# Router logits from split half-precision outputs, with the split done by ScalarE and GpSimd

## The reference

```python
x = x + xattn(layernorm(x), ctx, ctx)          # per token: 16 heads x 16 heads, causal, softmax
xf = layernorm(x).reshape(-1, D)
logits = xf @ gate_w.T + gate_b                # router, 8 experts
top1 = argmax(logits, axis=-1)
for e in range(8):
    h = relu(xf @ w1[e].T + b1[e]); y = h @ w2[e].T + b2[e]
    out = out + where(top1 == e, y, 0)
return x + out
```

## Time and profile before

| | |
|---|---|
| time, median of 3 runs | 470.85 us (469.33 to 471.26) |
| span of the profiled execution, first to last instruction | 462.9 us |
| what lies around the span, median less span | 7.95 us |
| busy: TensorE, VectorE, GpSimd, ScalarE | 384.6, 339.8, 207.6, 181.1 us |
| start to the first scores (L1403) | 27.3 us |
| last addition to `o_sb` (L1012) | begins at 227.16 us |
| expert tiles | about 229 to 455 us |

### The profile page before, as it was taken

The page is one execution under the profiler, slowest core; times in us unless marked ns, Lnnn a source line. Parts: engine busy times, 40 slices in busy tenths (PEclk is TensorE's granted clock), DMA queues, the critical chain, the costliest instruction groups (busy, mean ns, idle before and its releaser), DMA issues.

```text
span 462.9 us, 16301 instructions
## 1 busy us (share of the span) xinstructions
PE 384.6 (83%) x5889; PEld 328.5 (71%) x5889; DVE 339.8 (73%) x777; ACT 181.1 (39%) x317; POOL 207.6 (45%) x213
## 2 busy tenths in 40 slices
PE   0126878996798969895699999898999999999991
PEld 0026767996698869894688877676788888787870
DVE  8789799789882875378676987596867677766761
ACT  2344446454542523143353433243443434434320
POOL 8536444635673548643342354743333233233321
PEclk9999999955555555565589999999999999999998
DMA  7999989889778675667552544757543443434310
GB/s 264 417 254 236 264 220 260 260 188 240 200 161 218 159 160 112 180 141 219 125 143 67 107 98 106 186 139 184 106 94 99 95 108 90 104 84 106 100 29 0
DMA packets 125802, 73.17 MB, mean 158 GB/s; under 512 B 99229, under 2 KB 110238, under 8 KB 125216
## 3 DMA queue, kind: packets, MB, share of 16 engines
q1 hardware_dynamic: 96336, 60.46, 50.6%
q0 software_dynamic: 3408, 8.46, 5.0%
q10 hardware_dynamic: 25984, 3.21, 4.9%
HBM read 48.28 MB, written 11.24 MB: 129 GB/s over the span
## 4 chain that ended last, share of the span: by engine, by line
PE 58%; DVE 12%; issue 8%; SPq 7%; POOL 6%; DMA 5%; ACT 2%; POOLq 0%; DVEq 0%; ACTq 0%
PE s_ps L1506 19%; PE at_ps L1522 7%; PE pv_ps L1522 6%; PE s_ps L1403 6%; PE pv_ps L1433 5%; PE lg_ps L1459 4%; DMA arena<-qv_hl 3%; PE at_ps L1523 3%; PE pv_ps L1523 3%; SPq L601 3%; PE tr_ps L1445 2%; DVE arena L1186 2%; PE at_ps L1420 2%; POOL sorted_rows L1340 1%; POOL qv_hl L1296 1%
## 5 line engine op out<-in xcount | busy, mean ns | idle before, releaser
L1506 PEld LDWEIGHTS s_ps<-arena 128*128 x1872 | 131.9, 99 | 43.4 <-issue 4.9
L1506 PE MATMUL s_ps<-arena 128*128 128x128 f16 x1872 | 157.0, 221 | 2.8 <-issue 1.2
L1203 DVE SCALAR_TENSOR_TENSOR arena<-arena,s_ps 128x512 f32<-128x512 f32 x78 | 53.5, 685 | 32.5 <-PE s_ps L1506 21.1
L1433 PE MATMUL pv_ps<-a_hl,arena 128*128 128x16 f16 x1536 | 54.6, 180 | 17.1 <-DMA arena<-qv_hl 12.3
L1433 PEld LDWEIGHTS pv_ps<-a_hl,arena 128*128 128x128 f16 x1536 | 53.3, 118 | 20.7 <-DMA arena<-qv_hl 16.7
L1366 POOL DMA_INDIRECT result<-arena x39 | 38.9, 996 | 64.4 <-DVE arena L1228 60.3
L1403 PEld LDWEIGHTS s_ps<-k_hl,arena 128*128 128x128 f16 x1536 | 54.5, 118 | 15.4 <-DMA arena<-qv_hl 10.6
L1522 PE MATMUL at_ps<-arena,k_in 128*128 x160 | 60.3, 379 | 2.8 <-DVE k_hl L1214 2.8
L1359 POOL TENSOR_TENSOR arena<-arena 128x256 f32<-128x256 f32 x39 | 29.5, 756 | 73.4 <-DMA arena<-b 73.3
L1403 PE MATMUL s_ps<-k_hl,arena 128*128 128x16 f16 x1536 | 54.2, 180 | 9.7 <-DMA arena<-qv_hl 9.7
L1522 PE MATMUL pv_ps<-arena,x_in 128*128 x152 | 57.6, 379 | 0.0
(11 more groups left out here) (141 smaller groups left out, 589.9 us busy)
## 6 DMA issues: line engine op xcount, KB each, us to landing
arena<-w SPq DMA_DIRECT2D x28, 512.0 KB, 5.1
arena<-sorted_rows SPq DMA_DIRECT2D x39, 130.0 KB, 2.2
arena<-b SPq DMA_DIRECT2D x39, 128.0 KB
arena<-qv_hl SPq DMA_DIRECT2D x70, 64.0 KB
k_in<-k_t SPq DMA_DIRECT2D x16, 256.0 KB
arena<-x SPq DMA_DIRECT2D x4, 1024.0 KB, 10.6
x_in<-x_t SPq DMA_DIRECT2D x16, 256.0 KB, 5.0
v_in<-v_t SPq DMA_DIRECT2D x16, 256.0 KB
```

The source lines that it names most:

```text
L1203: eng.scalar_tensor_tensor(out=h_in[:, c].rearrange("p (k t) -> p k t", t=P), in0=bias, scalar=W_SCALE, in1=h_ps[c][:].rearrange("p (k t) ...
L1433: m = eng.matmul(o[:, n], v_bd[i][:, n // 2, :, n % 2, v], a_hl[:, n, a, :], start=(n, a, v) == (0, 0, 0), stop=(n, v) == (BLK - 1, 1))
L1506: k = eng.matmul(o, weights_of(j, w + k_ * H + n * P, P), xt[:, j % XB, a + k_], start=(k_, w, a) == (0, HI_1, 0), stop=k_ == KD - 1 and w ...
```

## The change

The float32 products of `gates` become products of half-precision (float16) parts. The gate's weights are scaled by 64 and split into high and low (`gate_hl`, VectorE), and GpSimd makes `gate_bd` from both in a step of its own (`gate_blocks`). Each chunk of `o_sb` is split into `o_hl`: ScalarE copies the high part, GpSimd subtracts to get the low part. Both walk the chunk head by head, so they read float32 numbers 64 bytes apart and write float16 numbers 4 bytes apart. TensorE does three products for each head instead of one. The wait of ScalarE's split on the group before's logits takes the place of SP's: `load_residual` now waits for the two splits. `sel` is made by a product of two inputs instead of a copy. The scaling is undone in `choose`. The software DMA queue's scratch in on-chip memory is set to 2048 bytes for each partition. The order of all steps that were there before is kept; the new ones are put in behind `outputs`.

```diff
 "ACT":
+  "output_halves": (5316, 6999, 7544, 7821, 10139, 11102, 11887, 12396, 14641, 15353, 16633, 16750, 19138, 19643, 20641, 20747),
 "POOL":
+  "gate_blocks": (2900,),
+  "output_halves": (5386, 7069, 7614, 7891, 10209, 11172, 11957, 12466, 14711, 15423, 16703, 16820, 19208, 19713, 20711, 20817),
-        gate_bd = sb("gate_bd", [P, HEADS, 8, E])
+        gate_bd = sb("gate_bd", [P, HEADS, 2, 8, E], F16)
+        gate_hl = sb("gate_hl", [P, 2, HEADS * E], F16)
+        o_hl = sb("o_hl", [P, HEADS, P, 2], F16)
@@ load_residual (SP)
-                    sp.wait_ge(s_logits, i // CG)
+                    sp.wait_ge(s_o_hi, i - CG + 1)
+                    sp.wait_ge(s_o_lo, i - CG + 1)
@@ ScalarE
+            def output_halves():
+                for i in range(NC):
+                    at = slice(i % CG * BLK, (i % CG + 1) * BLK)
+                    yield
+                    act.wait_ge(s_o, i + 1)
+                    act.wait_ge(s_logits, i // CG)
+                    eng.copy(o_hl[:, :, at, 0], o_sb[:, at, :].rearrange("p t h -> p h t")).then_inc(s_o_hi, 1)
@@ constants (VectorE)
-                eng.tensor_copy(sel[:], turn_of[:].unsqueeze(2).to_broadcast([P, 8, HD])).then_inc(s_select, 1)
+                eng.tensor_tensor(sel[:], turn_of[:].unsqueeze(2).to_broadcast([P, 8, HD]),
+                                  turn_of[:].unsqueeze(2).to_broadcast([P, 8, HD]), ALU.mult).then_inc(s_select, 1)
-                dve.wait_ge(s_select, 3)
-                eng.tensor_tensor(gate_bd[:], ... , ALU.mult).then_inc(s_gate_bd, 1)
+                eng.tensor_scalar(gate_hl[:, 0], gate_sb, W_SCALE, None, ALU.mult).then_inc(s_gate_hl, 1)
+                dve.wait_ge(s_gate_hl, 1)
+                eng.scalar_tensor_tensor(out=gate_hl[:, 1], in0=gate_sb, scalar=W_SCALE, in1=gate_hl[:, 0], op0=ALU.mult,
+                                         op1=ALU.subtract).then_inc(s_gate_hl, 1)
@@ GpSimd
+            def gate_blocks():
+                yield
+                pool.wait_ge(s_select, 3)
+                pool.wait_ge(s_gate_hl, 2)
+                for n in range(2):
+                    eng.tensor_tensor(gate_bd[:, :, n], gate_hl[:, n]... , owner[:]... , ALU.mult).then_inc(s_gate_bd, 1)
+            def output_halves():
+                for i in range(NC):
+                    at = slice(i % CG * BLK, (i % CG + 1) * BLK)
+                    hi, lo = [o_hl[:, :, at, n] for n in range(2)]
+                    yield
+                    pool.wait_ge(s_o_hi, i + 1)
+                    eng.tensor_tensor(lo, o_sb[:, at, :].rearrange("p t h -> p h t"), hi, ALU.subtract).then_inc(s_o_lo, 1)
@@ gates (TensorE)
-                            pe.wait_ge(s_gate_bd, 1)
-                            pe.wait_ge(s_o, CG * (g + 1))
+                            pe.wait_ge(s_gate_bd, 2)
+                            pe.wait_ge(s_o_hi, CG * (g + 1))
+                            pe.wait_ge(s_o_lo, CG * (g + 1))
-                            m = eng.matmul(LG, o_sb[:, :, h], gate_bd[:, h].rearrange("p b e -> p (b e)"), start=h == 0,
-                                           stop=h == HEADS - 1)
+                            for a, w in ((0, 0), (0, 1), (1, 0)):
+                                m = eng.matmul(LG, o_hl[:, h, :, a], gate_bd[:, h, w].rearrange("p b e -> p (b e)"),
+                                               start=(h, a, w) == (0, 0, 0), stop=(h, a) == (HEADS - 1, 1))
-    nc = bacc.Bacc("TRN2", target_bir_lowering=False, num_devices=1)
+    nc = bacc.Bacc("TRN2", target_bir_lowering=False, num_devices=1, dynamic_dma_scratch_size=2048)
```

More of the change, by code:

```diff
@@ L532, in xattn_moe_kernel @@
             ("s_o_t", "s_x1", "s_bn", "s_var1", "s_rstd1", "s_ln1", "s_logits", "s_eighths", "s_gate_cols", "s_gate_sum", "s_gate_bd")]
+        s_gate_hl, s_o_hi, s_o_lo = [sem(n) for n in ("s_gate_hl", "s_o_hi", "s_o_lo")]
         s_hot, s_seen, s_ranked, s_slot, s_tail = [sem(n) for n in ("s_hot", "s_seen", "s_ranked", "s_slot", "s_tail")]
@@ L888, in _ @@
             weave(TIMES["ACT"], spread_first_queries=spread_first_queries(), spread=spread(), queries=queries(),
-                  keys=keys(), values=values(), turned_rows=turned_rows(), exponentials=exponentials(),
+                  keys=keys(), values=values(), turned_rows=turned_rows(), output_halves=output_halves(),
+                  exponentials=exponentials(),
                   weights=weights(), expert_inputs=expert_inputs(), relus=relus())
@@ L912, in constants @@
                 yield
-                dve.wait_ge(s_select, 3)
                 dve.wait_ge(s_gate, 32)
-                eng.tensor_tensor(gate_bd[:], gate_sb.rearrange("p (h e) -> p h e", e=E).unsqueeze(2)
-                                  .to_broadcast([P, HEADS, 8, E]), owner[:].unsqueeze(1).unsqueeze(3)
-                                  .to_broadcast([P, HEADS, 8, E]), ALU.mult).then_inc(s_gate_bd, 1)
+                eng.tensor_scalar(gate_hl[:, 0], gate_sb, W_SCALE, None, ALU.mult).then_inc(s_gate_hl, 1)
+                dve.wait_ge(s_gate_hl, 1)
+                eng.scalar_tensor_tensor(out=gate_hl[:, 1], in0=gate_sb, scalar=W_SCALE, in1=gate_hl[:, 0], op0=ALU.mult,
+                                         op1=ALU.subtract).then_inc(s_gate_hl, 1)
                 yield
@@ L988, in softmax @@
                     dve.wait_ge(s_turned, i)
-                    dve.wait_ge(s_gate_bd, 1)
+                    dve.wait_ge(s_gate_hl, 2)
                     dve.wait_ge(s_gate_cols, 1)
@@ L1047, in choose @@
                     dve.wait_ge(s_logits, g + 1)
-                    eng.tensor_tensor(v[0], lg, pay[:, :, D + 1:D + 2].to_broadcast([P, G, E]), ALU.mult).then_inc(s_hot, 1)
+                    eng.scalar_tensor_tensor(out=v[0], in0=lg, scalar=1.0 / W_SCALE,
+                                             in1=pay[:, :, D + 1:D + 2].to_broadcast([P, G, E]), op0=ALU.mult,
+                                             op1=ALU.mult).then_inc(s_hot, 1)
                     yield
@@ L1305, in weights_of_softmax @@
                                       ALU.mult).then_inc(s_a, 1)
+            def gate_blocks():
[3 more added lines that the diff above has]
+                for n in range(2):
+                    eng.tensor_tensor(gate_bd[:, :, n], gate_hl[:, n].rearrange("p (h e) -> p h e", e=E).unsqueeze(2)
+                                      .to_broadcast([P, HEADS, 8, E]), owner[:].unsqueeze(1).unsqueeze(3)
+                                      .to_broadcast([P, HEADS, 8, E]), ALU.mult).then_inc(s_gate_bd, 1)
+            def output_halves():
[5 more added lines that the diff above has]
+                    eng.tensor_tensor(lo, o_sb[:, at, :].rearrange("p t h -> p h t"), hi, ALU.subtract).then_inc(s_o_lo, 1)
             def tables():
@@ L1373, in _ @@
                   values=values(), weights_of_softmax=weights_of_softmax(), tables=tables(),
+                  gate_blocks=gate_blocks(), output_halves=output_halves(),
                   layer_norms=layer_norms(), row_tails=row_tails(), scatters=scatters(),
```

## The result

The changed kernel takes 475.81 us (median of 4 runs, 475.41 to 476.71) against 471.06 us (4 runs, 469.33 to 472.35) of the kernel before in the same session: ratio 1.0131, interval 1.0086 to 1.0176. Forecast were 477.7 us and a slower kernel. The profiled execution of the changed kernel has a span of 473.8 us.

What follows compares the result with a forecast made beforehand. TensorE was taken to lead in the first group, GpSimd's queue and its DMA in the second. Terms 0.6 + 0.8 - 2.4 + 3.25 + 0.8 + 3.0 + 0.8 = +6.9 us gave 477.7 us, own range 472 to 483, 80% range 463.5 to 484.

Steps and rivals of the forecast that it cites:

- Rival 3: Whole kernel: TensorE is the bound all along and GpSimd's steps find pauses; -8 us, 463 us, chance 0.24.
- Rival 5: Software DMA queue: its smaller scratch holds the indirect DMAs, up to 30 us; about 485 us, chance 0.05.
- rival 4: GpSimd's low parts: the strided read is dearer than any row, 3 us a step; +17, 488 us, chance 0.06.
- p: Length of one low-part subtraction on GpSimd, taken as 1.7 us, bounds 1.17 to 2.13.
- The start: Before the first scores: shorter gate_bd work on VectorE, -0.9, and the query split 1.5 later; together +0.6 us.
- the copy to `sel`: At the start, 5.11 us ending at 10.78: its replacement by a two-input product was given nothing, bound -2.0.
- Chunk 0 and group 1: Chunk 0's low part delays the next spread DMAs, +0.8; in group 1 TensorE's faster logits give -2.4 us.
- Group 2: Low parts of chunks 5, 6 and 7 delay GpSimd's last scatter and ScalarE's copy by 4.35; less 1.1, +3.25 us.
- Chunk 9 and group 3: Chunk 9's low part holds the softmax product at 167.61, +0.8; chunks 10 and 11 around the query split, +3.0 us.
- Chunks 1, 2, 4, 8, 12 and 13: Their low parts fall in GpSimd pauses of 1.9 to 3.6 us; if these closed, 1.7 us each.
- Chunks 10 and 11: Group 3: low parts around the query split at 182.27 make scatters and value split 3.4 later; +3.0 us.
- Group 4 and the rest: Last group's logits wait 5.2 us, holding the first expert tile; four blocks give 4.4 back, +0.8 us.

Runs made afterwards that it cites:

- e11: Changed kernel with the low parts moved from GpSimd to VectorE, same layout and order numbers; 471.83 us, ratio 0.9993 to the kernel before.
- e10: Changed kernel where GpSimd makes all low parts but TensorE neither waits for nor uses them, the gate's low part counted twice; 479.59 us, ratio 1.0196.
- e3: Changed kernel without splits: products read upper bfloat16 halves of `o_sb`, outputs' low part left out, gate's counted twice; 461.92 us, ratio 0.9806.
- e6: Kernel before with only the software DMA queue's scratch set to 2048 bytes; 462.09 us, ratio 0.9936.
- e4: Changed kernel with GpSimd's gate blocks moved out of the start, from order number 2900 to 4900; 474.55 us, ratio 1.0124.
- e2: Changed kernel with both splits made but read by nobody, logits again float32 products of `o_sb` with float32 `gate_bd`; 480.56 us, ratio 1.0264.
- e12: Changed kernel with low parts on VectorE, `o_hl` packed in the order of `o_sb`, and gate blocks made later; 466.32 us, ratio 0.9937.
- e5: Changed kernel with TensorE's logits of the last three groups moved some 550 order numbers back; 475.74 us, ratio 1.022.
- e1: Changed kernel with `o_hl` in the order of `o_sb`: splits read and write 4 bytes apart, TensorE loads 64 bytes apart; 471.58 us, ratio 1.0057.

## Why the prediction was right, and where it was not

**The verdict: right, its mechanism in the main.** The low parts on GpSimd are what makes the kernel slower, as the forecast had it. e11 shows it: the same work done by VectorE takes away all of the 1.2 points. They cost in two ways, by GpSimd's queue, which the forecast had, and by holding VectorE, which it had only at the start; e11 takes both away at once, so the runs do not divide the price between them. e10 shows that the wait for the low part as such is not the price. Rival 3 (TensorE is the bound all along, -8 us) is near what the products do alone: -9.1 us by e3's ratio. Its condition, low parts in pauses, is the part that failed. Rival 5 (scratch) falls with e6, rival 4 (p = 3 us) with L1341.

**The prices of single steps.** The low part was taken at 1.7 us and has a median of 1.53, inside the bounds. The rule of the Trainium skill that the prediction weighed (GPSIMD Engine Reference, section "Performance pitfalls for Q7 kernels": half as much again for steps over 8 bytes) is given there for kernels of one's own on the Q7 cores; for the built-in subtraction with one such input these runs show a fifth: 1.28 us became 1.53. The measurement decides. ScalarE's step was taken at 0.8 and is 1.09, within its bound of 1.3; a block of products was 0.6 and is 0.73 in the mean, 0.51 us at full clock (at 251.76) and 0.80 where the granted clock is near 0.5 (at 243.69).

**The start: +0.6 forecast, +1.5 at the first mark.** Right were the query split (32.04 to 33.49, forecast +1.5) and the blocks (3.8 us, forecast 4.6). Wrong was the copy to `sel`, given nothing: as a product it takes 0.28 us instead of 5.11, and the first statistics come at 13.85 instead of 16.02. The two gate halves cost 0.67 and 1.14 us, not 0.5 together. On VectorE the gain still reaches 25.94, where L968 starts 1.7 us earlier than its counterpart at 27.67 before, and ends there. It does not reach the first scores: they start at 27.92 us, and between 27.20 and 28.18 in every run here, against 27.30 before, each time after a wait for the spread DMAs (12.46 us in the changed kernel, 9.66 before). That bound the forecast did not have. GpSimd and VectorE from 20 to 36 us in the changed kernel:

```profile
25.87 3.81 POOL L1331 TENSOR_TENSOR gate_bd<-gate_hl,owner 128x1024 f16<-128x1024 f16 x2
33.49 1.27 POOL L1301 TENSOR_TENSOR qv_hl<-x_in,qv_hl 128x512 f16<-128x512 f32 x1 [3.82 <-ACT qv_hl L793]
...
25.94 1.88 DVE L968 SCALAR_TENSOR_TENSOR xstat<-xbn,xstat 128x8 f32<-128x8 f32 x1 [1.54 <-POOL xstat L1294]
28.07 2.15 DVE L1205 SCALAR_TENSOR_TENSOR arena<-arena 128x512 f16<-128x512 f32 x1
```

The step L968 has 8 numbers a partition and took 0.17 us at this place before; started 0.07 us after a block, it ends with it, and the weight split behind it is held by the second. e4, with the blocks later, reaches the first mark 1.35 us earlier.

**Chunk 0 and group 1: -1.6 forecast, -0.3 measured.** The products alone give the 2.2 us there (e3) that the forecast followed through to -2.4. It costed the four low parts of the group at almost nothing, since they fall in pauses of GpSimd or in front of work that had time; e2 shows +1.3 for the splits.

**Group 2: +3.25 forecast, +3.3 measured.** The step by step reading was right, with p near enough and with the claim that TensorE's saved blocks only fill a wait (e2's and the changed kernel's group 2 are equal). The last scatter, its DMA and the copy to `pay`, which answer to the earlier trace rows:

```profile
144.28 4.08 DMA sorted_rows<-pay,slot_i
148.47 0.59 ACT pay L849
```

**Chunk 9 and group 3: +3.8 forecast, +6.2 measured. This is the step that failed most**, namely "Chunks 1, 2, 4, 8, 12 and 13 fall in pauses of GpSimd" and so cost nothing, and "+0.8" for chunk 9. Chunk 8's low part does fall in a pause of GpSimd. GpSimd and VectorE, changed kernel:

```profile
164.77 1.51 POOL L1341 TENSOR_TENSOR o_hl<-o_sb,o_hl 128x512 f16<-128x512 f32 x1
173.05 1.53 POOL L1341 TENSOR_TENSOR o_hl<-o_sb,o_hl 128x512 f16<-128x512 f32 x1 [3.11 <-ACT o_hl L858]
174.93 1.06 POOL L1323 TENSOR_TENSOR a_sb<-a_sb,inverse 128x512 f32<-128x512 f32 x1 [0.36 <-DVE inverse L1017]
...
165.16 3.22 DVE L1205 SCALAR_TENSOR_TENSOR arena<-arena 128x512 f16<-128x512 f32 x2
168.31 0.68 DVE L1020 TENSOR_TENSOR a_hl<-at_ps,a_hl 128x512 f16<-128x512 f32 x1
...
173.08 1.52 DVE L1044 TENSOR_SCALAR bn<-bn 128x8 f32<-128x8 f32 x1
```

VectorE, same place, kernel before:

```profile
161.09 1.27 DVE L1186 SCALAR_TENSOR_TENSOR arena<-arena 128x512 f16<-128x512 f32 x2
162.29 0.68 DVE L1003 TENSOR_TENSOR a_hl<-at_ps,a_hl 128x512 f16<-128x512 f32 x1
```

The same two weight splits take 3.22 us beside chunk 8's low part and the key split after it, and took 1.27. The split of the attention weights (`a_hl`) comes 1.5 us later, counted from the mark, and TensorE waits 3.86 us for it where a DMA had held it 2.34. At 173.08 it happens again: a step of 8 numbers, 0.17 us in the median before, takes 1.52, as long as chunk 9's low part beside it, and the reciprocal and the softmax product follow behind. Counted from the mark at 152.47, the softmax product behind chunk 9's low part (at 174.93; 167.61 before) is 2.8 us late and not 0.8. Chunks 10 and 11 then cost 2.3, and chunks 12 and 13, forecast at nothing, 1.1. (The forecast's 3.0 for chunks 10 and 11 does not follow from its own terms: 3.4 less 1.1 and 0.5 is 1.8.) So the low part takes its time twice, on GpSimd and from VectorE. That VectorE is held for the whole of GpSimd's step is what the equal lengths show (1.52 and 1.53 us here, 1.88 beside a block of 1.9 at the start). SBUF — State Buffer of the Trainium skill, section "🔬 SBUF: two separate sides", has this as a lock of a port pair that the two engines share: a VectorE step in a two-port mode, or with two inputs on chip against a GpSimd step that reads there, waits for the whole of it. The trace agrees on both sides: the additions of L1029, which read one input from TensorE's accumulators, keep their median of 0.67 us and never exceed 0.69, even where they fall wholly beside a low part (at 81.20), and the two-input product for `sel` runs in 0.28 us at 5.67, beside a memset, which reads nothing, where the copy at 5.67 had been held 5.11.

How much of the 6.2 us the held steps make was not tried by itself. With the low parts on VectorE that same softmax product comes no earlier: 22.2 us (e11) and 22.4 (e12) after the mark, as in the changed kernel (22.5), against 19.7 in the kernel before and 20.6 in e6. There VectorE spends the time on the low part itself, held once beside a query split. So at this place it is VectorE that sets the pace, and the low part costs its time there on either engine; what e11 and e12 give back lies in group 2 and behind chunks 10 and 11 (0.4 and 0.7 us there instead of 2.3).

**Group 4 and the rest: +0.8 forecast, +0.2 measured**, within what this stage varies by. The wait at the last logits is 7.0 us, 5.2 forecast. e5 and e10 show that taking this wait away at TensorE gains nothing: TensorE then waits for the last scatter of the third group, one step further on.

**Span and time.** The forecast put 7.95 us around the span and the runs show 1.8; the rest is that the profiled execution was quicker than the runs whose median was taken. Against that execution the sum should have been +10.9, not +6.9. The two errors have opposite signs, and that 477.7 us lies so close to 475.8 is luck: by the medians the change costs 4.75 us, less than either sum, and which stages carry those 4.75 the traces cannot say.

## What to carry over

A new step on GpSimd that finds a pause there is not free: look at what VectorE runs in the same microseconds, since its short steps and its splits with two inputs on chip can be held for as long as GpSimd's step lasts. Try giving such a step to VectorE instead (0.73 us against 1.28 here in the median) even where VectorE is the busier engine; it is not free there either, since GpSimd can hold it too (1.80 us at 159.24 in e12). Taking away a wait of TensorE is worth nothing while what it waits for next comes at the same time, and it can cost clock: after a stand of 5.6 us TensorE worked until 260 us at 0.53. And before the time around a span is taken from a median, it is compared with the run that the profile was made of.

## What the runs showed of the hardware beyond that

- Reading float32 64 bytes apart, with float16 written 4 bytes apart: GpSimd 1.28 to 1.53 us for 512 numbers, ScalarE 0.78 to 1.09, VectorE 0.73 to 1.03.
- Loading weights for TensorE from float16 64 bytes apart instead of 4 made the 192 products 14.3 us instead of 11.7 (e1 against the changed kernel).
- The same program takes 464.4 to 471.3 us in the median by session, and 460.3 to 473.3 in single runs; the changed kernel 473.5 to 476.7. What makes the kernel before vary more is open.
